# A recurrent network's set-up in another order, with two waits between its weight loads

## The reference, cut to what matters

```python
rp = concat([region_tbl[region_idx], poi_tbl[poi_idx]], -1)            # 8 + 4 values of each step
nv = concat([rp @ W_rp + b_rp, coords @ W_co + b_co], -1)              # 40
conv = elu(conv1d(nv, conv_w, 3 taps) + conv_b)                         # 8 steps of 32
emb = tanh(concat([car_tbl[car_idx], week_tbl[week_idx], time_tbl[time_idx]], -1))   # 27 values
x = concat([conv, emb at every step], -1)                               # 59
h = lstm_layer(x, Wih0, Whh0, bih0, bhh0)   # g = x @ Wih.T + h @ Whh.T + b; i, f, gg, o = split(g)
h = lstm_layer(h, Wih1, Whh1, bih1, bhh1)   # c = sig(f)*c + sig(i)*tanh(gg); h = sig(o)*tanh(c)
return ((h[:, -1] @ W1 + b1) @ W2 + b2) @ W3 + b3                       # 2048 x 512, float32
```

## Time and profile before

| what | value |
|---|---|
| median of three runs | 1106.76 us (1102.08 to 1108.24) |
| the profiled execution, its time | 1104.99 us |
| its span, first to last instruction | 1103.2 us |
| PE busy | 1067.3 us, 97% of the span |
| DVE, ACT, POOL busy | 742.3, 510.6 and 321.5 us |
| chain that ended last | PE 89%, DVE 4%, another core or an unknown queue 2%, issue 2% |
| data moved | 22.59 MB, a mean of 20 GB/s |

### The profile page before, as it was taken

How to read it: one execution, slowest core, us unless ns; L and a number is a source line. 1 busy time by engine, 2 the same in 40 slices (tenths; PEclk the granted TensorE clock), 3 DMA queues, 4 the chain that set the end, 5 groups by cost and what they waited for, 6 DMA issues and landing times.

```text
span 1103.2 us, 14328 instructions
## 1 busy us (share of the span) xinstructions
PE 1067.3 (97%) x4899; PEld 510.1 (46%) x4899; DVE 742.3 (67%) x1148; ACT 510.6 (46%) x738; POOL 321.5 (29%) x338
## 2 busy tenths in 40 slices
PE   5599999999999999999999999999999999999998
PEld 4555444444445444444445444444444544444444
DVE  3478877656877767567676848676586758666553
ACT  1255454435554544345555534444455544444432
POOL 6650045542440035552450025562441000000000
PEclk9799999999999999999999999999999999999999
DMA  9510001000010001000010101000010101000000
GB/s 249 124 18 15 1 3 32 2 2 1 2 31 19 21 5 31 3 2 1 2 31 1 39 4 31 3 2 1 2 31 1 39 1 29 1 0 1 1 1 38
DMA packets 32168, 22.59 MB, mean 20 GB/s; under 512 B 20239, under 2 KB 24423, under 8 KB 32103
## 3 DMA queue, kind: packets, MB, share of 16 engines
q1 hardware_dynamic: 20848, 20.53, 6.7%
q0 software_dynamic: 9984, 1.12, 2.5%
q10 hardware_dynamic: 1271, 0.08, 0.1%
HBM read 11.21 MB, written 4.19 MB: 14 GB/s over the span
## 4 chain that ended last, share of the span: by engine, by line
PE 89%; DVE 4%; another core or an unknown queue 2%; issue 2%; DMA 1%; SPq 1%; ACT 1%; DVEq 0%; ACTq 0%
PE acc L1355 51%; PE acc L1346 28%; PE acc L1337 5%; PE aux L1457 2%; DMA w_nat<-in_L_rec_Whh 1%; PE aux L1205 1%; PE aux L1270 1%; DVE row_max L871 1%; SPq L443 1%; PE aux L1304 1%; PE aux L1447 0%; DVE neg_part L1009 0%; DVE gates L1036 0%; ACT gates L747 0%
## 5 line engine op out<-in xcount | busy, mean ns | idle before, releaser
L1355 PE MATMUL acc<-h_part,wh 128*128 128x512 f16 (+1 forms) x2688 | 656.1, 380 | 1.6 <-DVE h_part L1087 1.6
L1355 PEld LDWEIGHTS acc<-h_part,wh 128*128 128x128 f16 x2688 | 245.0, 98 | 322.0 <-issue 55.9
L1346 PE MATMUL acc<-h_part,wh 128*128 128x512 f16 (+1 forms) x1488 | 358.5, 379 | 0.0
L747 ACT ACTIVATE gates<-acc,gate_bias,unscale 128x512 f32<-128x512 f32 x254 | 195.7, 776 | 313.5 <-PE acc L1355 275.0
L747 ACT ACTIVATE gates<-gates,gate_bias,unscale 128x512 f32<-128x512 f32 x242 | 189.3, 811 | 150.8 <-DVE gates L1036 142.5
L1346 PEld LDWEIGHTS acc<-h_part,wh 128*128 128x128 f16 x1488 | 144.6, 98 | 177.1 <-issue 6.2
L570 POOL DMA_INDIRECT feat<-in_L_rec_region_tbl,region_idx x160 | 162.5, 1016 | 165.0 <-PE acc L1355 128.1
L1036 DVE TENSOR_TENSOR gates<-acc,emb_gates 128x512 f32<-128x512 f32 x242 | 160.7, 686 | 51.1 <-PE acc L1355 38.1
L570 POOL DMA_INDIRECT feat<-in_L_rec_poi_tbl,poi_idx x120 | 121.5, 1013 | 115.2 <-PE acc L1355 96.6
L1337 PE MATMUL acc<-x_in,wx 96*128 96x512 f32 (+1 forms) x248 | 137.4, 560 | 3.5 <-ACT gates L747 2.0
L1083 DVE TENSOR_TENSOR h_full<-gates,tanh_c 128x512 f32<-128x512 f32 x120 | 82.6, 689 | 75.3 <-ACT tanh_c L752 70.9
(11 more groups left out here) (149 smaller groups left out, 349.9 us busy)
## 6 DMA issues: line engine op xcount, KB each, us to landing
out<-y SPq DMA_DIRECT2D x16, 256.0 KB, 2.1
x_in<-conv_hi SPq DMA_DIRECT2D x56, 64.0 KB
feat<-in_L_rec_region_tbl,region_idx POOLq DMA_INDIRECT x160
w<-in_L_rec_W SPq DMA_DIRECT2D x2, 1024.0 KB
w_nat<-in_L_rec_Whh SPq DMA_DIRECT2D x2, 1024.0 KB
w<-in_L_rec_W SPq DMA_DIRECT2D x1, 2048.0 KB
feat<-in_L_rec_poi_tbl,poi_idx POOLq DMA_INDIRECT x120
x_in<-conv_lo SPq DMA_DIRECT2D x28, 64.0 KB
```

The costliest lines, as they stand in the source:

```text
L747: nc.scalar.activation(gates[layer][:, j, g, :], source, ACT.Tanh if g == GATE_G else ACT.Sigmoid, bias=gate_bias[:, layer, m:m + 1], scal ...
L1346: mm = nc.tensor.matmul(bank, wh[:, 1, a, c, rows], h_part[0][:, s.write_slot, b, c, :], start=(c == 0 and a == b == HI), stop=(s.first an ...
L1355: mm = nc.tensor.matmul(bank, wh[:, own_w, a, c, rows], h_part[layer][:, s.read_slot, b, c, :], start=False, stop=(c == HK - 1 and a == LO))
```

## The change

Only the set-up and the opening cell are changed; the loop over the batches is as it was.

- SP's order is new, and it waits twice for landing: for the first batch's coordinates ahead of Wih1 and Whh1, and for Whh1 ahead of W3 and all that follows. The biases now stand behind Whh1, and W1 and the small indices are issued by ACT, the projection's matrices by SP.
- The POI indices come as 10 rows of 512 (`poi_flat`, one DMA). PE spreads them over the partitions with five half-precision matmuls (`spread_poi`), and DVE compares each of the five banks with the partition's number.
- The scales are multiplied into the weights (ACT, `scale_rows`, eight instructions for a matrix; DVE for Wih0), and the diagonals are gone: PE turns with plain transpositions.
- The opening cell uses DVE's sums like all others (6 sums more, 6 matmuls fewer). PE runs eight matmuls of no use at the start (`WARM_UP`).
- `product_head(0)` is cut in two halves with `turn_wh(1)` between them; DVE finds layer 1's row maxima and scales ahead of `put_band` and the input matrix's low parts, not behind them.

```diff
+            load_w2(0)
             load(w_nat[0][:, :, :], d["Whh0"].rearrange("(m p) k -> p m k", p=P), w_in[0])
...
+            load(wx_nat[:, :, 0:D_X], d["Wih0"].rearrange("(m p) k -> p m k", p=P), wx_in)
+            load_w2(1)
...
+            load(coords[:, 0:GR, :], coord_rows[:, 0:GR, :], coords_in)
+
+            sp.wait_ge(coords_in, DMA)
+            for i, k in ((1, "Wih1"), (2, "Whh1")):
+                load(w_nat[i][:, :, :], d[k].rearrange("(m p) k -> p m k", p=P), w_in[i])
...
-            load(wx_nat[:, :, 0:D_X], d["Wih0"].rearrange("(m p) k -> p m k", p=P), wx_in)
-            coord_rows = d["r_coords"].rearrange("(g p) t c -> p g (t c)", p=P)
-            load(coords[:, 0:GR, :], coord_rows[:, 0:GR, :], coords_in)
-            for i, k in ((1, "Wih1"), (2, "Whh1")):
-                load(w_nat[i][:, :, :], d[k].rearrange("(m p) k -> p m k", p=P), w_in[i])
+            sp.wait_ge(w_in[2], DMA)
             load(w3[:, :, :], d["W3"].rearrange("(k p) n -> p k n", p=P), w3_in)
...
+            def scale_rows(i, begin=0, end=M):
+
+                layer = 0 if i == 0 else 1
+                act.wait_ge(prep, (4, 9)[layer])
+                for m in range(begin, end):
+                    nc.scalar.activation(w_nat[i][:, m, :], w_nat[i][:, m, :], ACT.Copy,
+                                         scale=row_scale[:, layer, m:m + 1]).then_inc(w_scaled[i], 1)
...
+            scale_rows(0, 0, M // 2)
+            put_w12(4)
+            scale_rows(0, M // 2, M)
+            put_w12(5)
             put_proj()
...
-            diagonal1()
+            scale_rows(1)
+            put_wh_hi(1)
+            emb_tanhs(0, acc[:, 0, :])
             put_head_hi(0)
...
+                for i in range(POI_PIECES):
+                    dve.wait_ge(poi_spread_acc, i + 1)
+                    nc.vector.tensor_scalar(columns[:, i * NCOL:(i + 1) * NCOL], spread_bank(i), poi_number[:, 0:1], None,
+                                            ALU.is_equal).then_inc(poi_hot_put, 1)
...
                 if s.first and layer == 0:
-                    if not s.opening:
-                        sums(s, 0)
+                    sums(s, 0)
...
-                        mm = nc.tensor.matmul(aux[:, WH_BANKS[i][a], b * P:(b + 1) * P],
-                                              w_nat[i][:, m, k * P:(k + 1) * P], diag[layer][:, m, :],
-                                              start=True, stop=True)
+                        mm = nc.tensor.transpose(aux[:, WH_BANKS[i][a], b * P:(b + 1) * P],
+                                                 w_nat[i][:, m, k * P:(k + 1) * P], ident[:, :])
...
+            def spread_poi(begin, end):
+
+                pe.wait_ge(poi_spread_ready, 1)
+                pe.wait_ge(poi_row_put, 1)
+                for i in range(begin, end):
+                    if i == 3:
+                        pe.wait_ge(small_put, 1)
+                    elif i == 4:
+                        pe.wait_ge(poi_hot_put, 1)
+                    nc.tensor.matmul(spread_bank(i), poi_spread[:, i, :], poi_row[:, :], start=True, stop=True
+                                     ).then_inc(poi_spread_acc, 1)
...
-                            if s.opening:
-                                mm = nc.tensor.matmul(bank, we[:, rows], emb_in[:, :], start=False, stop=True)
...
+            product_w12(0)
+            turn_small()
+            product_w12(1)
+            spread_poi(0, 4)
+            product_w12(2)
+            product_w12(3)
+            spread_poi(4, POI_PIECES)
+            product_w12(4)
+            product_w12(5)
+            pe.wait_ge(poi_hot_put, POI_PIECES)
+            turn_proj()
+            poi_rows()
+            for m in range(6, K2):
                 product_w12(m)
-            turn_proj()
             turn_biases()
-            for m in range(4, K2):
-                product_w12(m)
             band()
...
-            product_head(0)
+            product_head(0, 0, K2 // 2)
+            turn_wh(1, [(wh_lo_put, 3), (first_turned_put, 1), (wh_lo_put, 4), (relu_done, 1)])
             pe.wait_ge(emb_copied, 1)
             turn_emb(acc[:, 0, :])
-            turn_wh(1, [(wh_lo_put, 3), (first_turned_put, 1), (wh_lo_put, 4), (relu_done, 1)])
+            product_head(0, K2 // 2, K2)
```

More of the change, by code:

```diff
@@ L739, in cell_acts @@
                         count = s.tile + s.place(j, g) + 1
-                        if layer == 0 and not s.opening:
+                        if layer == 0:
                             act.wait_ge(gate_sum, count)
@@ L1096, in cell @@
                     update_c(s, layer, 0)
-                    if not s.opening:
-                        sums(s, 1)
+                    sums(s, 1)
                     update_c(s, layer, 1)
@@ L1335, in cell @@
                             pe.wait_ge(acc_read[before_layer], before_end + (place - 3))
+                            if s.follows_opening and place == HK:
+                                pe.wait_ge(turned_put[0], 1)
                         if layer == 0:
[L1337 to L1340 removed]
+                            mm = nc.tensor.matmul(bank, wx[:, rows], x_in[:, s.t, :], start=True, stop=s.first)
                         else:
@@ L1360, in _ @@
             pe.wait_ge(ident_ready, 1)
-            turn_small()
+            for _ in range(WARM_UP):
+                nc.tensor.matmul(aux[:, 2, 0:P], ident[:, :], ident[:, :], start=True, stop=True)
             pe.wait_ge(w1_in, DMA)
```

236 lines of the change are left out of this document (116 added, 120 removed).

## The result

The changed kernel took 1100.66 us (median of 6 runs, 1099.2 to 1101.19) beside 1103.87 for the kernel before, a ratio of 0.996 with a 95% interval of 0.9943 to 0.9977. It is 0.4% faster, where 2.1% was forecast. The profiled execution took 1101.19 us.

What follows compares the result with a forecast made beforehand. PE, busy 97% of 1103.2 us, was taken as the bound, with a hole in the set-up. Gains 15.3 + 3.0 + 3.3 + 1.4 + 1.8 = 24.8, less 2, gave 23 and 1083 us; range 1077 to 1100 (8 in 10).

Steps and rivals of the forecast that it cites:

- the 23 us: Whole predicted gain, mostly in the set-up: terms summing to 24.8 us, less 2 for what is left of the hold.
- the hold costs 0 to 2: In the set-up, the first gap in the loads frees ACT and DVE, leaving a delay of 0 to 2 us.
- Rival (2): The gaps do nothing and the hold of ACT and DVE ends with the loads at 38.5: 1101 us; chance 0.17.
- The sentence on instruction refills: ACT's and DVE's set-up hold might be an instruction refill over DMA, not mostly hidden: 17.8 us of DVE.
- The 15.3 us: In the set-up, turning the input matrix starts at 29.7 us instead of 44.98.
- from there to T0: From the input matrix's turn to the first conv_pair's start: 3.0 us shorter than 11.0, bounds 0 to 3.6.
- T0 to the opening cell: From the first conv_pair's start to the opening cell: 3.3 us shorter than 16.7, bounds 1.0 and 4.
- opening cell to the second: In the opening cell, 12 matmuls become 6, saving 1.4 us; DVE's six sums stay hidden under product_head(1).
- turn_wh(2): On PE's path at 96.72 us, turning takes half of 3.73: 1.8 us saved, bounds 0 and 1.8.
- the clock's 1.8 us: Between the first conv_pair and the opening cell, PE regains 1.8 us lost to a lower clock after the hole.
- Rival (1): Only the second gap in the loads, 27 to 28.5 us, frees ACT and DVE: 8.5 us later, 1091; chance 0.15.
- rival (3): The hold catches DVE ahead of put_small and PE stands until 38.5: 1107 us, or 1111; chance 0.05.

Runs made afterwards that it cites:

- experiment 3: Changed kernel with SyncE's first wait lengthened: layer 1's loads and all behind them held until the last copy of W1 x W2; 1113.23 us, ratio 1.0065.
- experiment 4: Changed kernel with GpSimd's first indirect gathers held until the last copy of W1 x W2, bulk loads running as before; 1121.09 us, ratio 1.0125.
- experiment 14: Changed kernel without SyncE's two waits and with b1 loaded right behind W1; 1100.9 us, ratio 0.9941 (kernel before 1106.81).
- experiment 12: Changed kernel with GpSimd waiting for landing after each four gathers; 1098.44 us, ratio 0.9915 (kernel before 1106.81).
- experiments 5 and 7: Changed kernel with a landing wait after each four gathers: 1097.5 us with SyncE's two waits, 1093.64 without them (kernel before 1085.17).
- experiment 15: Changed kernel without SyncE's two waits, b1 loaded right behind W1, and a landing wait after each eight gathers; 1092.24 us, ratio 0.9856.

## Why the prediction was wrong, point by point

The step that failed is the reading on which the 23 us rested: "I read this as a hold that lasts as long as the loads run without a gap", and with it "So both engines are held" and "the hold costs 0 to 2". ACT and DVE were free and waited for signals of TensorE, which are late in these sessions while GpSimd issues gathers closely one behind the other: with the loads stopped (experiment 3), and not with the loads running and the gathers held (experiment 4). The pauses at 33 and 20 GB/s freed nobody for good, and the hold cost 17.5 us and not 0 to 2: the input matrix is turned at 50.07, against 32.54 where no signal is late. Nor did it begin where I had counted, at ACT's third scaling and DVE's second or third pass, but ahead of them, at ACT's copy at 19.76 and DVE's first pass. Rival (2) gave the time, 1101, and a right consequence (the pauses gain nothing), by a wrong mechanism: in experiment 3 the signals were still late with the loads stopped. The coincidence that misled me, 39.5 with the end of the loads at 39.6, was one with the gathers as well: the last is issued by 35.5, and POOL goes on with their rows at 39.8, after 4.1 us of waiting for the landing. That end I had not looked at. The sentence on instruction refills falls with it. By the Trainium skill's rule on turns between queues (DMA: Bandwidth & Descriptors, "Queues, rings and completion order"), which I had weighed against the forecast, a gap would not end the hold. The trace agrees: the hold outlasts both gaps, until 40.83.

A second error lay under it. The 15.3 us were booked as a gain of the change. They are the price of the late signals in the kernel before: in the prompt session it turns the input matrix at 29.04, sooner than the 29.7 that I had forecast for the changed kernel. Term by term in us (minus is gained; measured on PE's timelines, of both kernels in each kind of session):

| term | predicted | late | prompt |
|---|---|---|---|
| start of turning the input matrix | -15.3 | +5.1 (44.98 to 50.07) | +3.5 (29.04 to 32.54) |
| from there to T0 | -3.0 | -4.0 (11.0 to 7.0) | -3.2 (9.3 to 6.1) |
| T0 to the opening cell | -3.3 | -3.2 (16.7 to 13.5) | -3.3 (16.8 to 13.5) |
| opening cell to the second | -1.4 | -0.2 | -0.2 |
| turn_wh(2) | -1.8 | -1.8 | -1.8 |
| behind it | 0 | +0.3 | +1.4 |
| span | | -3.8 | -3.6 |

The prompt column is of the two profiled executions, which are 3.6 us apart; the medians are 1.9 apart. The profiled execution of the changed kernel was among the fastest of its eleven, that of the kernel before 0.6 above the median.

- *PE up to T0.* Where no signal is late T0 is 38.64, and I said 37.7. The turn comes 2.8 us later than forecast (32.54, not 29.7). The term that was mis-sized is DVE's `put_small`: I had it let the fourth piece of `spread_poi` go at 14.8, and the piece starts at 17.45. DVE begins Whh0's maxima only at 13.87, behind its steps on `poi_flat`, whose landing it awaits until 10.91. PE also waits 3.53 us for b1, whose load the change moved behind the small indices on ACT's queue and to which I had given no term; products 0 and 1 end at 16.3 and not at 12.2. But DVE's copy comes later still: with b1 early the fourth piece starts at 17.09 (experiment 14), so that b1 costs 0.4 us on this path. Against the kernel before, the +3.5 is 2.0 at the end of product 3 (21.5 against 19.5), 1.1 for `poi_rows`, which now lies ahead of the turn, and 0.4 for the fifth piece and the rest. In the late session the last late signal comes 1.4 us later than before (40.87 against 39.52). Behind it the changed kernel still has `poi_rows` and two products, slow at first since the granted clock is 0.50 from 43.1 to 45.0 (5.6 us instead of 3.7), where the kernel before has three passes of DVE.
- *From there to T0* and *T0 to the opening cell*: near in size, with the 4.0 of the late session above my bound of 3.6. For the second, the clock's 1.8 us hold in the late session, in which `product_head` takes 8.83 us before and 3.70 + 3.60 now:

```profile
56.58 8.83 PE L1270 MATMUL acc<-w,w_t 128*128 128x512 f32 x16
```

In the prompt session both kernels have a clock of 1.00 there and the gain is the same, for another reason: 1.9 for half of turn_wh(1) and idle PE time of 1.12 and 1.03 us, the second for a `wh` piece that is late behind DVE's maxima, against 1.0 us of new small gaps.
- *Opening cell*: mis-sized, 0.2 instead of 1.4. The six matmuls take 2.6 us instead of 2.8. DVE copies `emb_gates` until 53.0, so its first sum ends at 53.7. PE's fifth matmul waits for it (0.58 at 53.80), and the last two take 0.94 us. I had looked at DVE's load over the whole stretch and not at the place where a bank is asked for.
- *turn_wh(2)*: right. Some is given back behind it: 0.69 for DVE's sums at 93.17 and 0.42 for ACT before, 1.1 of the 1.4 us.
- Rival (1) and rival (3) did not come. DVE's `put_small` was late by its own work and by no signal.

The forecast of 1083 agrees with the 1083.55 us of the prompt session. That is no credit: the kernel before takes 1085.5 there, so the change is worth 1.9 us and not 23.

*Open:* what makes a session late (the same chips gave both); by what path a run of gathers delays TensorE's signals; whether it is their issuing or their transfers; and what brings the signals back, fewer gathers in a run or more time behind it. Waits by four do it with some 5 us behind each of the first three runs (experiment 12) and don't with 1.6 (experiment 4). The pauses cost 3.9 us with waits by four (experiments 5 and 7) and nothing that could be measured without them in late sessions; alone in a prompt session they were not tried.

## What to carry to other kernels

A wait without a releaser is put to the test by asking whose signal it waits for: if all such waits on several engines ask for the same engine, its signals are the first suspect, and a signal in the other direction that arrives on time supports it. Before a hole is put down to one of two things that run beside it, look at the end of each, and stop one in an experiment; it takes one wait. A hole in the kernel before is no gain of the change until something in the change is shown to close it.

## What the runs showed of the hardware

- TensorE's signals came up to 19.1 us late while GpSimd issued 24 indirect gathers of 128 rows, one every 1.25 us, with the DMA engines at 4 GB/s (experiment 3). With a wait for landing after each four, of some 5 us for the first three, they were on time (experiment 12). With waits of 1.6 us after each four, behind a run of 24, ACT still stood 12.9 us (experiment 4). With eight in a row they were up to 5.4 us late (experiment 15).
- Whether this happens changes from one batch of runs to another on the same chip, and why is open: the same kernel took 1085.2 and 1106.3 us on one chip, 1085.5 and 1106.8 on another, with every run of a batch of one kind.
- The cheapest cure measured is one wait for landing between the second and the third step's gathers and one ahead of the embeddings', in the kernel before: 1106.3 to 1090.6 us. What it costs there in a prompt session was not measured; in the changed kernel it cost 1.6 us.
